# Attention weights transposed in two halves of 64 rows, two units at a time

## The reference

```
q, k, v = x Wq', x Wk', x Wv'        # 32 query heads, 8 key heads, head size 128
q, k = rope(rmsnorm(q)), rope(rmsnorm(k))
keys = 512 cached (16 pages of 32 tokens, named by a table) + the 32 own ones
scores = q . keys / sqrt(128); cached keys from the sequence's length on are masked
o = softmax(scores) . values;  x = x + o Wo'
x = x + (x W1' + gated low-rank experts);  x = x + (x W2' + b + adapter);  x = x + adapter
```

## Time and profile before

| | before |
|---|---|
| median of 3 runs | 2462.41 us |
| the profiled execution | 2462.17 us |
| its span | 2460.4 us |
| mean granted TensorE clock | 0.996 |
| PE busy | 2421.6 us, 98% |
| DVE busy | 1590.0 us, 65% |
| ACT busy | 1241.2 us, 50% |
| POOL busy | 767.9 us, 31% |

### The profile page before, as it was taken

How to read it: one execution, slowest core, us unless ns; L and a number is a source line. 1 busy time by engine, 2 the same in 40 slices (tenths; PEclk the granted TensorE clock), 3 DMA queues, 4 the chain that set the end, 5 groups by cost and what they waited for, 6 DMA issues and landing times.

```text
span 2460.4 us, 48713 instructions
## 1 busy us (share of the span) xinstructions
PE 2421.6 (98%) x14960; PEld 2093.3 (85%) x14960; DVE 1590.0 (65%) x4346; ACT 1241.2 (50%) x3212; POOL 767.9 (31%) x854
## 2 busy tenths in 40 slices
PE   8999999999999999999999999999999899999998
PEld 7877777778899999999999999999998788888886
DVE  5777777774577777777777777777776333343333
ACT  4777777775455555555555555555555222222221
POOL 5666666665123333332222212122211211111111
PEclk9999999999999999999999999999999999999999
DMA  6233233334998888888888988888887233333331
GB/s 217 68 105 103 87 102 98 91 103 132 328 332 279 281 279 285 281 281 280 283 282 285 287 286 285 282 284 286 288 285 240 85 106 97 104 102 98 99 103 47
DMA packets 390754, 488.60 MB, mean 199 GB/s; under 512 B 53536, under 2 KB 325152, under 8 KB 387616
## 3 DMA queue, kind: packets, MB, share of 16 engines
q1 hardware_dynamic: 353696, 351.89, 45.5%
q0 software_dynamic: 36864, 134.23, 16.6%
HBM read 397.89 MB, written 88.08 MB: 198 GB/s over the span
## 4 chain that ended last, share of the span: by engine, by line
PE 74%; POOL 10%; issue 7%; ACT 4%; DVE 2%; SPq 2%; DMA 1%; POOLq 0%; DVEq 0%; ACTq 0%
PE s_bank L1019 19%; PE o_bank L1033 18%; POOL q_t L498 7%; PE pt_a L1073 5%; PE pt_b L1073 4%; PE proj L1521 4%; PE proj L1523 4%; PE proj L1522 4%; ACT normed L562 3%; PE o_bank L1057 3%; POOL w_hi L458 2%; POOL w_lo L460 1%; PE acc L728 1%; PE acc L729 1%; PE acc L730 1%
## 5 line engine op out<-in xcount | busy, mean ns | idle before, releaser
L935 ACT ACTIVATE probs<-probs,neg_max 128x544 f32<-128x544 f32 x512 | 383.3, 749 | 567.5 <-DVE neg_max L985 567.5
L1019 PE MATMUL s_bank<-k_t,q_t 128*128 128x288 f32 (+1 forms) x2048 | 557.1, 394 | 3.8 <-DVE neg_max L985 2.8
L1033 PEld LDWEIGHTS o_bank<-p_t,v_c 128*128 128x128 f32 x4096 | 537.4, 192 | 26.4 <-DVE p_t L955 0.2
L985 DVE CUSTOM_DVE_ANT_0 probs<-s_bank,mask 128x544 f32<-128x544 f32 x512 | 370.9, 724 | 282.8 <-PE s_bank L1019 278.7
L1033 PE MATMUL o_bank<-p_t,v_c 128*128 128x128 f32 x4096 | 539.7, 275 | 0.0
L1019 PEld LDWEIGHTS s_bank<-k_t,q_t 128*128 128x128 f32 x2048 | 349.1, 190 | 64.5 <-DVE neg_max L985 10.2
L138 POOL DMA_INDIRECT v_c<-in_v_rows,v_row x256 | 249.1, 973 | 320.7 <-PE o_bank L1033 279.8
L728 PE MATMUL acc<-w_hi,x_hi 128*128 128x512 f32 x764 | 314.9, 412 | 0.0
L498 POOL TENSOR_TENSOR q_t<-normed,v_c 128x256 f32<-128x256 f32 x320 | 248.9, 798 | 182.7 <-ACT normed L562 180.8
L729 PE MATMUL acc<-w_lo,x_hi 128*128 128x512 f32 x764 | 301.4, 394 | 0.0
L730 PE MATMUL acc<-w_hi,x_lo 128*128 128x512 f32 x764 | 300.2, 393 | 0.0
(11 more groups left out here) (158 smaller groups left out, 3868.4 us busy)
## 6 DMA issues: line engine op xcount, KB each, us to landing
k_t<-in_k_pages SPq DMA_DIRECT2D x1024, 128.0 KB
q_spill<-wo_early SPq DMA_DIRECT2D x32, 1024.0 KB, 5.2
q_t<-q_spill SPq DMA_DIRECT2D x64, 512.0 KB
o_spill<-o_t SPq DMA_DIRECT2D x64, 512.0 KB, 6.7
raw<-o_spill SPq DMA_DIRECT2D x64, 512.0 KB, 3.5
k_t<-in_w_qkv SPq DMA_DIRECT2D x11, 1024.0 KB, 8.2
v_spill<-wo_early SPq DMA_DIRECT2D x8, 1024.0 KB, 7.5
k_spill<-wo_early SPq DMA_DIRECT2D x8, 1024.0 KB, 5.1
```

The lines of the kernel that those rows point to most:

```text
L935: nc.scalar.activation(probs[:, j % SLOTS_P], probs[:, j % SLOTS_P], ACT.Exp, scale=-1.0, bias=neg_max[:, j % 2:j % 2 + 1], accum_out=row_ ...
L985: nc.vector.tensor_tensor_reduce(out=probs[:, j % SLOTS_P], in0=s_run, in1=mask[:, par], scale=-SCALE, scalar=3.0e38, op0=ALU.add, op1=ALU ...
L1019: last = pe.matmul(s_bank[:, columns].rearrange("p (s t) -> p s t", t=PSIZE), q_t[:, par, g], k_t[:, par, slots, g], start=True, stop=True)
L1033: last = pe.matmul(o_of(n), v_c[:, par, c, g * HD:(g + 1) * HD], p_t[:, i, c], start=opens_bank(n) and c == 0, stop=False)
```

## The change

The weights of two units are transposed together. Each block of 128 x 128 becomes two transposes with 64 rows each, the lower half to `pt_a`, the upper to `pt_b`, so that DVE and ACT now copy 64 of the 128 columns of all four blocks. PE's program is written for two units: score n, weigh n-6 and half of n-5, score n+1, the rest of n-5, then transposes of n-2 and n-1, with the own transpose, where there is one, ahead of them. `p_t` has four slots. LAG is 4. ACT, no longer DVE, scales the own columns, after the exponential of the next unit. The mask of a sequence is built at the last unit of the one before.

```diff
-    LOW = 2
-    LAG = 3
+    LAG = 4
+    WEIGH_AFTER = 6
+    SLOTS_T = 4
+    SIDE = P // 2
...
     (ACT)
             def pt_evacuate(n, i):
                 act.wait_ge(turned, n + 1)
-                at_least(act, summed, n - 1)
-                nc.scalar.activation(p_t[:, i, LOW:KC].rearrange("p c n -> p (c n)"), pt_b[i][:, 0:(KC - LOW) * ROWS],
+                at_least(act, summed, n - SLOTS_T + 1)
+                nc.scalar.activation(p_t[:, n % SLOTS_T, :, SIDE:P], pt_b[i][:, 0:KC * SIDE].rearrange("p (c n) -> p c n", c=KC),
                                      ACT.Copy).then_inc(pt_b_out, 1)
...
+            def normalise_own(n):
+                act.wait_ge(inverted, n + 1)
+                nc.scalar.activation(own[:, n // QUAD % 2, n % QUAD], probs[:, n % SLOTS_P, L:KEYS], ACT.Copy,
+                                     scale=inv_sum[:, n % 2:n % 2 + 1]).then_inc(own_normed, 1)
...
                     nc.scalar.activation(probs[:, j % SLOTS_P], probs[:, j % SLOTS_P], ACT.Exp, scale=-1.0,
...
+                    if n >= 1:
+                        normalise_own(n - 1)
...
     (DVE)
-                at_least(dve, summed, n - 1)
-                nc.vector.tensor_copy(p_t[:, i, 0:LOW].rearrange("p c n -> p (c n)"), pt_a[i][:, 0:LOW * ROWS])\
+                at_least(dve, summed, n - SLOTS_T + 1)
+                nc.vector.tensor_copy(p_t[:, n % SLOTS_T, :, 0:SIDE], pt_a[i][:, 0:KC * SIDE].rearrange("p (c n) -> p c n", c=KC))\
                     .then_inc(pt_a_out, 1)
...
             def invert(n, i):
                 dve.wait_ge(weighed, n + 1)
+                at_least(dve, own_normed, n - 1)
...
-                nc.vector.tensor_scalar(own[:, j // QUAD % 2, j % QUAD], probs[:, j % SLOTS_P, L:KEYS], inverse, None, ALU.mult)\
-                    .then_inc(normed, 1)
...
+                    at_least(dve, own_normed, n - SLOTS_P + 1)
                     dve.wait_ge(scored, n + 1)
...
+                    if g == HK - 1 and n < PAIRS * UNITS - 1:
+                        build_mask(n // HK + 1, 1 - par)
...
     (PE, transposes of one unit; its waits for pt_a_out and pt_b_out stay)
-                pe.wait_ge(normed, 2 * n + 2)
+                pe.wait_ge(normed, n + 1)
                 for c in range(KC):
-                    bank, at = (pt_a, c) if c < LOW else (pt_b, c - LOW)
-                    last = pe.transpose(bank[i][:, at * ROWS:(at + 1) * ROWS],
-                                        probs[:, n % SLOTS_P, c * P:(c + 1) * P], ident[:, :])
...
+                    for side, bank in enumerate((pt_a, pt_b)):
+                        rows = slice(side * SIDE, (side + 1) * SIDE)
+                        last = pe.transpose(bank[i][:, c * SIDE:(c + 1) * SIDE], probs[rows, n % SLOTS_P, c * P:(c + 1) * P],
+                                            ident[rows, rows])
                 last.then_inc(turned, 1)
+            def turn_pair(n):
+                if is_last(n + 1):
+                    turn_own(n + 1)
+                turn(n)
+                turn(n + 1)
...
             def emit(p, first):
-                for j in range(UNITS):
+                for j in range(0, UNITS, 2):
                     n = p * UNITS + j
                     score(n, p, j)
-                    if n >= LAG + 1:
-                        weigh_values(n - LAG - 1)
-                        if (n - LAG - 1) % HK == HK - 1:
-                            weigh_own((n - LAG - 1) // HK)
+                    if n >= WEIGH_AFTER:
+                        weigh_values(n - WEIGH_AFTER, 0, KC)
+                        weigh_values(n - WEIGH_AFTER + 1, 0, KC // 2)
+                    score(n + 1, p, j + 1)
+                    if n >= WEIGH_AFTER:
+                        weigh_values(n - WEIGH_AFTER + 1, KC // 2, KC)
+                        if (n - WEIGH_AFTER + 1) % HK == HK - 1:
+                            weigh_own((n - WEIGH_AFTER) // HK)
                     if n >= 2:
-                        turn(n - 2)
+                        turn_pair(n - 2)
```

More of the change, by code:

```diff
@@ L781, in attend @@
         inv_sum = sb("inv_sum", [P, 2])
-        p_t = sb("p_t", [P, 2, KC, ROWS])
+        p_t = sb("p_t", [P, SLOTS_T, KC, ROWS])
         own_t = sb("own_t", [P, QUADS, ROWS])
@@ L811, in attend @@
         inverted = sem("inverted")
-        normed = sem("weights_normed")
+        normed, own_normed = sem("weights_normed"), sem("own_weights_normed")
         turned = sem("weights_turned")
@@ L912, in pt_evacuate @@
                     at_least(act, own_summed, n // HK)
-                    nc.scalar.activation(own_t[:, n // QUAD % QUADS], pt_b[i][:, (KC - LOW) * ROWS:(KC - LOW + 1) * ROWS],
-                                         ACT.Copy).then_inc(own_out, 1)
+                    nc.scalar.activation(own_t[:, n // QUAD % QUADS], pt_b[i][:, KC * SIDE:KC * SIDE + ROWS], ACT.Copy)\
+                        .then_inc(own_out, 1)
+            def normalise_own(n):
+                act.wait_ge(inverted, n + 1)
+                nc.scalar.activation(own[:, n // QUAD % 2, n % QUAD], probs[:, n % SLOTS_P, L:KEYS], ACT.Copy,
+                                     scale=inv_sum[:, n % 2:n % 2 + 1]).then_inc(own_normed, 1)
             def o_evacuate(b, bank):
@@ L926, in emit @@
                     n = p * UNITS + j
-                    whole = n >= HK + QUAD and n % HK == QUAD
+                    whole = n >= HK + WEIGH_AFTER and n % HK == WEIGH_AFTER
                     if whole:
@@ L937, in emit @@
                                          accum_out=row_sum[:, j % 2:j % 2 + 1]).then_inc(weighed, 1)
+                    if n >= 1:
+                        normalise_own(n - 1)
             def tail(p):
                 n = p * UNITS
-                for m in (n - 3, n - 2, n - 1):
+                normalise_own(n - 1)
+                for m in range(n - LAG, n):
                     pt_evacuate(m, m % 2)
@@ L953, in pt_evacuate, with build_mask @@
                 dve.wait_ge(turned, n + 1)
-                at_least(dve, summed, n - 1)
-                nc.vector.tensor_copy(p_t[:, i, 0:LOW].rearrange("p c n -> p (c n)"), pt_a[i][:, 0:LOW * ROWS])\
+                at_least(dve, summed, n - SLOTS_T + 1)
+                nc.vector.tensor_copy(p_t[:, n % SLOTS_T, :, 0:SIDE], pt_a[i][:, 0:KC * SIDE].rearrange("p (c n) -> p c n", c=KC))\
                     .then_inc(pt_a_out, 1)
+            def build_mask(b, par):
+                nc.vector.tensor_scalar(mask[:, par, 0:L], key_index[:, :], seq_f[:, bass.ds(b, 1)], NEG,
+                                        ALU.is_ge, ALU.mult).then_inc(masked_in, 1)
             def invert(n, i):
                 dve.wait_ge(weighed, n + 1)
+                at_least(dve, own_normed, n - 1)
                 nc.vector.reciprocal(inv_sum[:, i:i + 1], row_sum[:, i:i + 1]).then_inc(inverted, 1)
@@ L973, in emit @@
                     dve.wait_ge(own_unmasked, 1)
+                    build_mask(0, 0)
                 for j in range(UNITS):
@@ L977, in emit @@
                     if g == 0:
[L979 to L982, removed]
+                        dve.wait_ge(masked_in, p * 2 + par + 1)
                     at_least(dve, turned, n - SLOTS_P + 1)
+                    at_least(dve, own_normed, n - SLOTS_P + 1)
                     dve.wait_ge(scored, n + 1)
@@ L993, in emit @@
                         normalise((j - 1) % UNITS)
+                    if g == HK - 1 and n < PAIRS * UNITS - 1:
+                        build_mask(n // HK + 1, 1 - par)
             def tail(p):
                 n = p * UNITS
-                pt_evacuate(n - 3, (n - 3) % 2)
                 invert(n - 1, 1)
@@ L1000, in tail @@
                 normalise(UNITS - 1)
-                for m in (n - 2, n - 1):
+                for m in range(n - LAG, n):
                     pt_evacuate(m, m % 2)
@@ L1021, in score, with weigh_values @@
                 last.then_inc(scored, 1)
[L1023 to L1033, removed]
+            def weigh_values(n, low, high):
+                par, g = n // HK % 2, n % HK
+                if low == 0:
+                    if g == 0:
+                        pe.wait_ge(v_in[par], 16 * KC * (n // UNITS + 1))
+                    if opens_bank(n):
+                        at_least(pe, o_out, 2 * (n // HK) - 1 + bank_of(n))
+                    pe.wait_ge(pt_a_out, n + 1)
+                    pe.wait_ge(pt_b_out, n + 1)
+                for c in range(low, high):
+                    last = pe.matmul(o_of(n), v_c[:, par, c, g * HD:(g + 1) * HD], p_t[:, n % SLOTS_T, c],
                                      start=opens_bank(n) and c == 0, stop=False)
-                last.then_inc(summed, 1)
+                if high == KC:
+                    last.then_inc(summed, 1)
             def bank_of(n):
@@ L1059, in weigh_own, with turn_own @@
                 last.then_inc(own_summed, 1)
+            def turn_own(n):
+                at_least(pe, pt_b_out, n - 1)
+                if n < UNITS:
```

(18 more changed lines are left out.)

## The result

| | before | after |
|---|---|---|
| median of the runs beside each other | 2462.65 us (4 runs) | 2571.1 us (2570.32 to 2572.86, 4 runs) |
| ratio, 95% interval | | 1.0438 [1.042, 1.0456] |
| span of the profiled execution | 2460.4 us | 2568.5 us |

What follows compares the result with a forecast made beforehand. TensorE, busy 98%, was taken to bound the kernel. Steps of 972.8 and 365.4 us, start 13.0 and end 7.5 made 1358.7 against 1255.2, +103.5: 2566 us, 4.2% slower; own range 2540 to 2595, wider 2515 to 2650.

Steps and rivals of the forecast that it cites:

- Pairs of half transposes: PE's transposes: two halves in different rows overlap, 0.06 us a pair, so a unit's four blocks take 0.24 instead of 0.44.
- Rival A: Transposes: pairs take 0.11 us, because loads bound them or halves don't run side by side; 2642 us, chance 0.17.
- What the halves are worth with their switches: Transposes alone: two units save 0.40 us and pay one 0.35 round trip; 13 us gained.
- The bank wait: PE before turn(n-1): waits for DVE's copy of n-3, which stands behind the masking of n+1; 0.60 us idle.
- T+1.43: Release of PE by DVE's copy: T is the end of PE's score slot, copy ends T+1.38, release takes 0.05.
- Steps: PE's step of two units takes 5.12 us, against 4.50 before; 5.80 where it holds weigh_own.
- The sum: Attention stage: 972.8 + 365.4 + 13.0 start + 7.5 end = 1358.7 us against 1255.2, +103.5.
- The start: First three steps of the stage: six scores 5.5, five gaps of 1.1, one of 1.95; 13.0 us.
- ScalarE: Scaling own columns on ACT: 512 more instructions of 0.19 to 0.27, 97 to 138 us, covered by its neg_max wait.
- The strided copy: Copies out of PSUM writing pieces of 64: taken as 0.42 us; 0.1 either way on DVE's is 19 us.
- The mask's new place: Mask moved to the end of the 8th unit: worth at most 13 us, nothing beside the new wait.
- B: Bank wait does not bite, as the copy ends by T+0.83; batch 19.23, -17 us, 2446 us; chance 0.10.

Runs made afterwards that it cites:

- e3: Kernel after with whole 128 x 128 transposes and DVE's copy of unit n-3 moved early, to the end of step n: 2459.57 us, ratio to before 0.9992.
- e1: Kernel after with DVE's copy of unit n-3 moved early, to the end of step n, ahead of the masking of n+1: 2448.87 us, ratio to before 0.9947.
- e2: Kernel after with whole 128 x 128 transposes instead of halves, DVE's copy left late: 2571.4 us, ratio to before 1.0448.
- e4: Kernel after with two useless float32 matmuls put before the transposes in each step without weigh_own: 2567.62 us, ratio to before 1.0426.
- e5: e1 with the own transpose moved ahead of weigh_own in the step that has both: 2433.27 us, ratio to before 0.9889.
- e7: Kernel before with half transposes alone, one unit at a time, own transpose ahead of the blocks, pt_b_out wait at first weighing matmul: 2512.2 us, ratio 1.0199.
- e6: e1 with the scaling of the own columns given back to VectorE: 2452.88 us, ratio to before 0.9959.

## Why the prediction was right

The forecast was 2566 us and the measured time is 2571.1. Step by step, by its own numbers:

1. *Pairs of half transposes.* Estimated 0.06 each; measured 0.06. The transpose loads behind L1057 were the right row, and L1552 the wrong one. Rival A, and with it the Trainium skill's rule that a load of 128 columns takes 107 ns (TensorE: Matmul & The Clock Gate, "LDWEIGHTS (loading the stationary operand)"), would need pairs 0.11 apart; the trace has 0.06 (1311.18 to 1311.24). What the halves are worth with their switches, 13 us estimated, is about 8 us in the stage and 10.7 by the medians (e3 against e1).
2. *The bank wait.* The release was put at T+1.43 with 0.60 us of idle time; it comes at T+1.46 (1312.05), and the idle time is 0.60 before this load and 0.56 on average (107.6 / 191). It appears in three steps of four and not behind weigh_own, as forecast. The count is 191 instead of 190, since the last of the three starting steps has it too. e1 shows that it is the cause, e2 that the halves are not, e4 that PE's own work is not what bounds. PE busy was forecast at about 94% and is 95%.
3. *Steps.* 5.12 and 5.80 predicted, 5.13 and 5.81 measured.
4. *The sum.* 1358.7 us for the stage; measured from the first score (634.14) to the end of the last weigh_own (1998.4 + 0.27) it is 1364.5. Of the 5.8 missing, 253 x 0.01 = 2.5 are the steps, and 0.5 stay unexplained. The start is 2.8: until the score of unit 6 it takes 15.8 us (634.14 to 649.94), where I had 13.0. The windows of the start show why (length, busy us of PE, PEld, DVE, ACT, POOL with counts, granted clock, DMA share, GB/s), of the kernel after and then of e2:

```profile
638.00:645.00 7.00, 5.75 (x25) 3.69 (x26) 3.52 (x12) 2.75 (x7) 0.00 (x0) 0.54 0.61 237
```
```profile
638.00:645.00 7.00, 5.21 (x24) 3.40 (x23) 4.50 (x14) 4.26 (x14) 0.00 (x0) 1.00 0.53 204
```

   TensorE ran most of these 7 us at the lower of its clocks, 1.2 GHz, in the kernel after, and at 2.4 in e2. From the first score to the first weighing it is 16.8 us there (634.14 to 650.96) and 14.3 in e2 (633.47 to 647.81); with the score of unit 6 I had 13.9. I had no term for the clock. Outside the stage two differences work against each other: it starts 1.1 us later than before (634.14 against 633.0), and what follows it is 2.4 us shorter (570.1 against 572.5), with the same program.
5. *ScalarE.* My bounds for the scaling of the own columns, 0.19 to 0.27 us, were too low. The new line takes 0.305:

```profile
L920 ACT ACTIVATE own<-probs,inv_sum x512: 304/305/322, 639.2 to 1991.4; 128x32 f32<-128x32 f32 x171
```

   That is 156 us of ACT and not at most 138. It was hidden all the same, as argued, since ACT waits 597.7 us for neg_max.
6. *The strided copy* keeps its length:

```profile
L965 DVE COPY p_t<-pt_a x512: 411/420/425, 646.9 to 1994.0; 128x256 f32<-128x256 f32 x171
```

7. *The mask's new place.* At most 13 us were put on it, and nothing beside the new wait. With the wait gone, e3 shows what it does: its loads wait for neg_max 4 times, 5.7 us, where before had 27 and 10.2. By the medians e3 gains 2.7 us, which the interval [0.9983, 1.0001] doesn't tell from none, and it differs from before by the order, the slots, the lag and ScalarE's share too.

The rival on the other side, B, asked for the copy to end by T+0.83 and gave 2446 us. e1 makes that condition true and measures 2448.87. B was wrong for this kernel only in where the copy stands. Its sum holds a slip: the batches 19.46 and 19.23 of the prediction are 0.23 apart, not 0.26, which gives 15 us and 2448. Its batch of 19.23 is 19.30 in e1.

One more wait could stand in e1: the next score's load begins at 1310.11, 0.12 behind the end of the neg_max read (1309.91 + 0.08). It costs next to nothing. The load begins 0.15 or 0.16 us behind the start of the last half transpose in all but one of 228 steps between 700 and 1800 us. In the kernel after, where the mask is long done by then, it is 0.15 too (1312.29 to 1312.44).

What stays open: why the clock falls at the start of the stage in some traces and not in others, and why the part behind the stage, the same program in all kernels, takes from 569.7 (e1) to 572.5 us (before). Differences of 2 us between kernels can come from there.

## What to carry to other kernels

When two pieces of work are put together on one engine, the second asks for its buffer one step sooner than before: look for the engine that frees it and read what stands ahead of the freeing in that engine's program, not how busy it is. A wait of this kind has a fixed end, counted from the event that starts the other engine's chain, so work saved or added ahead of it changes nothing as long as it fits into the gap (e4), and moving the freeing is worth all of it (e1: 122 us). Price a change of the array's arrangement by the round trip, and put all work of one arrangement side by side (e5: 0.30 us for each round trip taken away, 64 times).

## What the runs showed of the hardware

- Two half transposes in different rows run at once and need 0.06 us a pair, two loads of 128 columns and two moving sides of 64 included. Ordinary float32 loads of as many columns begin 0.11 apart. Whole float32 transposes have their loads 0.06 apart too, right behind weigh_own, and their records 0.11 apart in a row (e2). So a load for a float32 transpose lets the next one begin after about half the time of one for a float32 matmul.
- A round trip between whole and half rows costs some 0.3 us: taking one away saved 0.30 a batch (e5). The same 16 matmuls take 0.10 longer when whole rows follow (1.09 against 0.99 us). In e7 a unit gets 0.15 longer (2.25 to 2.40), though its four pairs save 0.20.
- At the start of the stage PE waits 0.8 to 1.2 us between scores. In five of the nine kernels the granted clock of 638 to 645 us then shows the lower level for most of the time (after 0.54, e3 0.58, e4 0.57, e5 0.55, e7 0.52), and in the others it stays at 1.00 (before, e1, e2, e6). Kernels with half and with whole transposes are on both sides, and in the kernel after and in e2 PE did the same just before: two scores with idle time between them. Each kernel has one trace, so whether it goes by kernel or by execution is not shown. From the first score to the first weighing e5 takes 16.2 us (632.93 to 649.14) and e1 13.7 (635.02 to 648.75), with the same program up to there: the lower clock costs 2.5 us, about 0.1%. The windows of e5 and e1:

```profile
638.00:645.00 7.00, 6.07 (x27) 3.47 (x25) 2.59 (x8) 2.62 (x9) 0.00 (x0) 0.55 0.48 184
```
```profile
638.00:645.00 7.00, 4.68 (x31) 2.69 (x29) 4.20 (x13) 3.55 (x12) 0.00 (x0) 1.00 0.75 290
```

- ACT takes 0.305 us for 128 x 32 scaled by a column, more than the 0.266 of a plain copy of 128 x 128 out of PSUM.
